# Router logits with the gate weights held in the array: two column halves, a turn back on TensorE, a sum on VectorE

## What is computed

```
x1 = layernorm(x + attention(x))              # 4096 x 512
scores = softmax(x1 @ gate_w.T, axis=-1)      # 4096 x 64: the logits are x1 @ gate_w.T
topk_w, topk_idx = top_k(scores, 6)
# tokens are put into slots of their experts in token order, at most 128 an expert
routed = scatter_add(expert(x1[buf_tok]) * buf_w)
out = layernorm(x1 + routed + shared(x1))
```

## Time and profile before

| what | value |
|---|---|
| median of 3 runs | 951.53 us (951.29 to 953.97) |
| span of the profiled execution | 945.2 us, 15175 instructions |
| PE busy | 918.1 us (97% of the span) |
| DVE busy | 683.3 us (72%) |
| ACT busy | 499.5 us (53%) |
| POOL busy | 460.9 us (49%) |
| mean granted TensorE clock | 0.994 |

### The profile page before, as it was taken

How to read it: one execution, slowest core, us unless ns; L and a number is a source line. 1 busy time by engine, 2 the same in 40 slices (tenths; PEclk the granted TensorE clock), 3 DMA queues, 4 the chain that set the end, 5 groups by cost and what they waited for, 6 DMA issues and landing times. The chain is left out here.

```text
span 945.2 us, 15175 instructions
## 1 busy us (share of the span) xinstructions
PE 918.1 (97%) x4626; PEld 727.5 (77%) x4626; DVE 683.3 (72%) x1250; ACT 499.5 (53%) x1015; POOL 460.9 (49%) x540
## 2 busy tenths in 40 slices
PE   9999999999999999998999999999999999999996
PEld 7788888888888888776787777777777677767875
DVE  7996878879797877987766666665655565636776
ACT  5543434344443535453456665666555566545775
POOL 2002456665656656677135445554545544433564
PEclk9999999999999999999999999999999999999998
DMA  7244735434342516275569999999999999969972
GB/s 209 89 155 121 176 90 158 117 108 132 125 127 75 177 59 204 79 268 173 174 196 302 308 322 322 321 316 318 322 287 307 305 305 303 322 113 392 382 259 111
DMA packets 114190, 203.91 MB, mean 216 GB/s; under 512 B 18496, under 2 KB 56384, under 8 KB 113088
## 3 DMA queue, kind: packets, MB, share of 16 engines
q1 hardware_dynamic: 93584, 159.87, 51.6%
q0 software_dynamic: 19520, 35.75, 16.7%
q10 hardware_dynamic: 1008, 7.34, 2.2%
HBM read 143.03 MB, written 59.88 MB: 215 GB/s over the span
## 5 line engine op out<-in xcount | busy, mean ns | idle before, releaser
L1535 POOL DMA_INDIRECT slot_table<-tokens,slot_of x162 | 181.0, 1118 | 86.7 <-issue 50.3
L1577 POOL DMA_INDIRECT acc_rows<-eo,table_sb x64 | 110.6, 1729 | 172.5 <-ACT eo L888 127.2
L1632 PE MATMUL bank<-x_hi,wqkv_hi 128*128 128x512 f32 x384 | 152.1, 396 | 0.3 <-DVE wqkv_lo L972 0.3
L1632 PE MATMUL bank<-x_hi,wqkv_lo 128*128 128x512 f32 x384 | 150.2, 391 | 0.0
L1632 PE MATMUL bank<-x_lo,wqkv_hi 128*128 128x512 f32 x384 | 150.2, 391 | 0.0
L1404 DVE TENSOR_TENSOR wgu_lo<-wgu,wgu_hi 128x1536 fp32r<-128x1536 f32 x64 | 112.4, 1758 | 48.0 <-ACT wgu_hi L882 48.0
L1632 PE MATMUL bank<-wdn,hid_et 96*128 96x512 f32 x256 | 122.8, 602 | 8.2 <-ACT hid_et L924 8.2
L882 ACT CAST wgu_hi<-wgu 128x1536 fp32r<-128x1536 f32 x64 | 94.5, 1477 | 5.8 <-DMA wgu<-w_gu 5.4
L1566 POOL DMA_INDIRECT xg<-x_rows,table_sb x64 | 74.3, 1162 | 41.3 <-DVE table_sb L1133 22.0
L1632 PE MATMUL bank<-wgu_hi,xgt_hi 128*128 128x384 f32 x256 | 91.4, 357 | 0.0
L1632 PE MATMUL bank<-wgu_hi,xgt_lo 128*128 128x384 f32 x256 | 85.9, 335 | 0.0
(11 more groups left out here) (183 smaller groups left out, 2146.0 us busy)
## 6 DMA issues: line engine op xcount, KB each, us to landing
wgu<-w_gu SPq DMA_DIRECT2D x64, 768.0 KB, 8.5
wdn<-w_down SPq DMA_DIRECT2D x64, 384.0 KB, 8.5
xres<-x SPq DMA_DIRECT2D x32, 256.0 KB, 2.9
x_turned<-x1t SPq DMA_DIRECT2D x32, 256.0 KB
x_rows<-x SPq DMA_DIRECT2D x32, 256.0 KB, 3.0
acc_rows<-x SPq DMA_DIRECT2D x32, 256.0 KB, 3.1
fin<-acc_rows SPq DMA_DIRECT2D x8, 1024.0 KB, 12.1
odd<-acc_rows SPq DMA_DIRECT2D x8, 1024.0 KB, 13.9
```

The source lines that it names most:

```text
L1535: pool.indirect_dma_start(table_dram, bass.IndirectOffsetOnAxis(slot_of[:, i, k:k + 1], 0), tokens[:, i:i + 1], None, bounds_check=SLOTS - ...
L1577: pool.indirect_dma_start(acc_dram[e % 2], bass.IndirectOffsetOnAxis(table_sb[:, e:e + 1], 0), eo[eo_slot[e]][:, :], None, bounds_check=T ...
L1632: mm = pe.matmul(out_ap, a, b, start=first and i == 0, stop=final and i == len(products) - 1)
```

## The change

The roles in `gate` are swapped: a piece of the gate weights (128 x 64) is held in one half of the array's columns and 128 columns of x1t stream through. Pieces 0 and 2 go to columns 0 to 63, pieces 1 and 3 to columns 64 to 127, and the result, 2 halves of 64 experts by 128 tokens, stands turned. ACT copies it to SBUF (`copy_gate`), PE turns it back (`turn_logits`, one transpose of 128 x 128, after project k of the next step), and DVE adds the halves into `logits` (a tensor_reduce, at the head of `top`). With that `top` moves from the end of a step into the next one, ahead of phi_k, and `route` from the start of that step to behind `run_kv`. `count_before` stays where it was. On ACT the exp of the logits becomes `soften`, behind the exp and relu of k, and `scale_score` goes to the end of the step.

```diff
 # PE
+            def turn_logits(i):
+                pe.wait_ge(gate_copied, i + 1)
+                pe.wait_ge(consts, C_IDENT)
+                if i:
+                    pe.wait_ge(logits_done, i)
+                pe.transpose(logits_ps(i), gate_out[:, :], ident[:, :]).then_inc(logits_mm, 1)
...
-                chain(small_ps[:, 0:E], [(x1t_sb[i % 2][:, k, :], gate_sb[:, k, :]) for k in range(KC)]).then_inc(score_mm, 1)
+                for k in range(KC):
+                    half = slice(k % 2 * E, (k % 2 + 1) * E)
+                    mm = pe.matmul(gate_ps[half, :], gate_sb[:, k, :], x1t_sb[i % 2][:, k, :], start=k < 2, stop=k >= KC - 2)
+                mm.then_inc(score_mm, 1)
...
                 project(s, it, c, 0, k_mm)
+                if before_tile is not None:
+                    turn_logits(before_tile)
                 mix(it, c, 0)
...
                 gate(i, 0)
                 if i + 1 < NT:
                     turn_x1(i + 1)
+                turn_logits(i)
                 unit()
 # DVE
             def top(i):
+                dve.wait_ge(logits_mm, i + 1)
...
+                dve.tensor_reduce(logits[:, 0:E], logits_ps(i).rearrange("p (h e) -> p e h", h=2), axis=AX.X, op=ALU.add).then_inc(logits_done, 1)
...
-                if before_tile is not None:
-                    route(before_tile)
                 if s:
                     numerator(s - 1)
                 if s and it + 1 < NB:
                     x_low(it + 1, c)
+                if before_tile is not None:
+                    top(before_tile)
...
                 if s == len(qk) - 1:
                     dve.wait_ge(head_send_done, 1)
+                if before_tile is not None:
+                    route(before_tile)
                 mix(it, c, 1)
...
                     place(before_tile)
-                if tile is not None:
-                    top(tile)
 # ACT
-            def copy_logits(i):
+            def copy_gate(i):
                 act.wait_ge(score_mm, i + 1)
-                act.wait_ge(consts, C_PADS)
                 if i:
-                    act.wait_ge(any_done, i)
-                act.copy(logits[:, 0:E], small_ps[:, 0:E]).then_inc(logits_done, 1)
+                    act.wait_ge(logits_mm, i)
+                act.copy(gate_out[:, :], gate_ps).then_inc(gate_copied, 1)
+
+            def soften(i):
                 act.wait_ge(top_done, i + 1)
...
-                if before_tile is not None:
-                    scale_score(before_tile)
                 if s and it + 1 < NB:
                     split_x(it + 1, c)
...
                 feature_parts(s, 0)
+                if before_tile is not None:
+                    soften(before_tile)
...
                 split_att()
+                if before_tile is not None:
+                    scale_score(before_tile)
                 if tile is not None:
-                    copy_logits(tile)
+                    copy_gate(tile)
```

More of the change, by code:

```diff
@@ L123, in build @@
     att_lo = att.place("att_lo", [P, KC, BT], F32R)
-    den = att.place("den", [P, P])
     rden = att.place("rden", [P, P])
@@ L131, in build @@
     rden_parts = att.place("rden_parts", [P, BT], F32R)
+    gate_out = att.place("gate_out", [P, P])
     logits = att.place("logits", [P, E + 2])
@@ L329, in build, with logits_ps @@
         proj_ps, turn_ps, rows_ps, small_ps, count_ps = banks[0:3], banks[3], banks[4], banks[5], banks[7]
+        gate_ps = banks[5][:, 0:P]
+        def logits_ps(i):
+            return turn_ps[:, 0:P] if i < LAST - 3 else small_ps[:, P:2 * P]
         send_ps = [banks[6], banks[4]]
@@ L840, in _ @@
             rden_high(NB - 1)
+            soften(LAST - 4)
             scale_score(LAST - 4)
             unit()
-            copy_logits(LAST - 3)
+            copy_gate(LAST - 3)
             split_shared(2, "d", sd_hi, sd_stage)
+            soften(LAST - 3)
             copy_turned(LAST - 2)
@@ L848, in _ @@
             split_att()
-            copy_logits(LAST - 2)
+            copy_gate(LAST - 2)
+            soften(LAST - 2)
             divided[0] += 2
@@ L857, in _ @@
             copy_turned(LAST - 1)
-            copy_logits(LAST - 1)
+            copy_gate(LAST - 1)
             apply_x1(LAST)
+            soften(LAST - 1)
             copy_turned(LAST)
@@ L863, in _ @@
             for i in range(LAST, NT):
-                copy_logits(i)
+                copy_gate(i)
                 if i + 1 < NT:
                     copy_turned(i + 1)
+                soften(i)
                 scale_score(i)
@@ L1352, in _ @@
                         split_x1t(0)
+            top(LAST - 4)
             numerator(STEPS - 1)
@@ L1661, in spread, with out_rows @@
                 pe.matmul(send_ps[part % 2][:, :], head_send[:, part, :], rden_parts[:, :], start=True, stop=True).then_inc(send_mm, 1)
-            def out_rows(i):
+            def out_rows(i, chunks=range(KC)):
                 b, j = divmod(i, NJ)
                 tok = slice(j * P, (j + 1) * P)
[L1666 to L1671, removed]
+                if 0 in chunks:
+                    pe.wait_ge(stage_lo, NSTAGE)
+                    if i:
+                        pe.wait_ge(x1_added, i)
+                    pe.wait_ge(div_done, KC * (b + 1))
+                for k in chunks:
                     pe.wait_ge(att_lo_done, KC * b + k + 1)
@@ L1674, in out_rows @@
                                first=k == 0, final=k == KC - 1)
-                mm.then_inc(out_mm, 1)
+                if KC - 1 in chunks:
+                    mm.then_inc(out_mm, 1)
             def sums(b, gated):
@@ L1815, in _ @@
             count_rest(LAST - 5)
+            turn_logits(LAST - 4)
             sums(NB - 1, LAST - 3)
@@ L1820, in _ @@
             gate(LAST - 3, NB)
+            spread(NB - 1, 0)
+            spread(NB - 1, 1)
+            turn_logits(LAST - 3)
             unit()
             count_rest(LAST - 4)
-            spread(NB - 1, 0)
-            spread(NB - 1, 1)
             count_before(LAST - 3)
@@ L1831, in _ @@
             spread(NB - 1, 3)
+            turn_logits(LAST - 2)
             unit()
@@ L1838, in _ @@
             gate(LAST - 1, 0)
-            out_rows(LAST + 2)
+            out_rows(LAST + 2, (0, 1))
+            turn_logits(LAST - 1)
+            out_rows(LAST + 2, (2, 3))
             count_before(LAST - 1)
```

24 lines of the change are left out of this document (16 added, 8 removed).

## The result

The changed kernel takes 991.96 us (median of 5 runs, 985.48 to 995.99), against 953.97 us for the kernel before, measured beside it (median of 5, the three runs of the table above among them): ratio 1.0382, 95% interval 1.0344 to 1.0420, slower. The ratio is taken over all the runs and not from the two medians. The profiled execution is the fastest of the five, 985.48 us with a span of 983.7, so that 1.8 us lie around the span.

The account below looks back on a forecast made before the run. PE, busy 918.1 of 945.2 us, was taken as the bound. Adding 21.6 for block waits, 0 for last tiles and 5 for clock gave a 971.8 us span; with 6.3 for the median, 978 us, range 966 to 996.

Parts of the forecast that it names:

- the sum: Whole kernel: span before 945.2, plus 21.6 for blocks, 0 for last tiles, 5 for clock, giving 971.8 us.
- rival 1: Both waits, and PE loses more: gate halves run serially or clock falls after c=1 too; 988 to 998 us, chance 0.20.
- The gate: Gate on PE: 0.64 us until the next matmul instead of 0.89, a gain of 0.25 us.
- The net gain: Gate's gain less the 0.12 us turn back on PE: 0.13 us a tile, 4.2 us for 32 tiles.
- c=1: Second step of a block: PE waits 1.73 us at count_before, as any_choice now comes behind run_kv.
- c=2: Third step of a block: PE waits 2.26 us more at count_before, between 1.36 and 2.88.
- c=0 and c=3: First and last steps of a block: any_choice is ready in time, so PE has no wait at count_before.
- The clock: Granted clock halves after three of six c=2 waits, costing 5 us (0 to 10).
- The tail: Closing loop: some 2.3 us wait at turn_logits(30) offset by a shorter wait at turn_x1(30); 0, 3 us either side.
- faster: At count_before: any_choice is ready whenever PE comes, and the gate's 4.2 us gain remains; 947 us, chance 0.04.
- VectorE catches up in c=2: DVE's stretch in c=2 shrinks to PE's 10.14 us, only the c=1 wait is left; 960 us, chance 0.10.
- the heavier case: Same as rival 1: serial gate halves (8 us) or clock falls after c=1 waits (up to 10 us); chance 0.20.

Follow-up runs that it names:

- route early: Changed kernel with route on VectorE moved back to right behind phi_k, ahead of run_kv; 960.7 us, ratio 1.0092 to the kernel before.
- route early with the old tail: Changed kernel with route back right behind phi_k, and tiles 25 to 31 using the gate and tail order of the kernel before; 953.04 us, ratio 0.9978.

## Why the prediction was right, and by how much it was off

The direction and the mechanism of the blocks held; the time was 14 us above the forecast of 978 and inside the range. The 14 can be told apart. The span of the profiled run is 11.9 us above the 971.8 of the sum: the blocks with their clock lost 27.25 for 26.6, the tail 13.0 for 0, the experts gave 1.8 back for 0. The run of the median, not profiled, has a span of 990.2, 6.5 more, at a clock of 0.979. Against that, the 6.3 us that were added for what lies around the span were 4.5 too many: here it is 991.96 - 990.2 = 1.8, and 2.0 to 3.5 in the 24 runs of the kernel before beside the last variants. So the first trace of before, with its span of 945.2, came from an execution of some 947 to 949 us, an estimate from these differences, which is faster than the median. 11.9 + 6.5 - 4.5 = 13.9.

That the range held it is in part luck: its high end had 3 us for the tail, and the 13.0 found room in waits of 2.88 us, six falls of the clock and 6 us of rival 1, which did not come in that measure.

- **The gate.** 0.59 us where 0.64 was worked out from `sums`, so the halves do run side by side. But the start behind `count_before` is 0.09 us later, and from `count_before` on the gain is 0.93 - 0.72 = 0.21, for 0.25. The Trainium skill (TensorEngine Tiling (Array Packing), Key Properties) says that changing the tiling mode drains the engine; the later start agrees with that. Its twofold figure (Theoretical Speedup) is not reached: 0.89 to 0.59 is 1.5, and 1.3 with the later start.
- **The net gain.** 0.13 us a tile were taken; route early shows 10.23 - 10.19 = 0.04 in c=1, and 52.01 us for a block (203.68 to 255.69) against 52.27, 0.065 a tile. The turn was priced right: from it to the next projection it is 329.72 - 329.38 = 0.34 with a `spread` between, and a `spread` alone takes 0.23 (311.31 to 311.54 in the trace of before), so 0.11 for 0.12. With the gate's 0.21 that leaves 0.10; where the rest goes isn't shown. Over 25 tiles 0.065 is 1.6 us; the ratio of route early with the old tail, 0.9978, allows from 0 to 4.
- **c=1.** Predicted 1.73 us from start to start; 1.65 in blocks 2, 4 and 7 (1.49 by the view, 1.48 in block 7). In blocks 3, 5 and 6, where the view gives 2.2 us, another thing comes in (last section). The chain was that of the forecast.
- **c=2.** Predicted 2.26 from a stretch of 12.4 us between the `run_kv` ends; it is 235.50 - 223.20 = 12.30, and the wait is 2.10 from start to start, 1.94 by the view in blocks 2, 4, 5 and 6 within 0.01. Block 3 has 1.73 and block 7 2.72.
- **c=0 and c=3.** No wait, as predicted. A block loses 3.45 us for 3.6; the 14 waits sum to 24.8 us for "some 12, about 24", and two of them, 1.5 us, are in the tail.
- **The clock.** Three falls after c=2 waits, as taken, but one also after a c=1 wait: four stretches of 3.4 us at half clock, 6.8 us lost where the term had 5. With two more stretches in the tail it is 8.1 over the span of the profiled run, and more in the others, whose clock is lower. The length of a wait alone does not decide it: of the 1.94 to 1.95 us of c=2, two kept the clock and two didn't.
- **The tail.** This is the step that failed. The working looked at tile 30 alone, and there it was right: PE waits 2.51 us (2.3 predicted) for the copy, which stands behind ACT's `hid_hi`, and the wait of 2.79 us at turn_x1(30) is gone.

```profile
487.74 0.66 PE L1751 MATMUL bank<-ident,x 128*128 128x128 f32 x4
490.90 0.34 PE L1774 MATMUL bank<-ident,gate_out 128*128 128x128 f32 x1 [2.51 <-ACT gate_out L719]
```

What it missed is tiles 25 and 26, whose turn stands behind their own gate with only two spreads (25), or a `count_rest` and two spreads (26), between. Of tile 26, in the trace of after:

```profile
448.39 0.66 PE L1766 MATMUL bank<-x1t,gate_sb 128*64 128x128 f32 x8
...
454.91 0.27 ACT L719 COPY gate_out<-bank 128x128 f32<-128x128 f32 x1 [6.75 <-remote]
...
455.23 0.47 PE L1774 MATMUL bank<-ident,gate_out 128*128 128x128 f32 x1 [5.49 <-issue]
```

ACT has nothing else to do, and yet copies the gate's result 5.86 us after the gate's last record ends (449.05). In the old tail a whole unit follows without a need for that result. From `count_before` of tile 25 to that of tile 26 it is 7.4 to 11.5 us in the five profiles with the old tail and 14.8 to 17.3 in the eight with the new gate there. How much of the 5.49 us PE really stood isn't shown: a late result of this kind comes in the kernel before as well (last section). So 0 was taken for a tail that costs some 8.5 us on one chip, and 13.0 between the two first profiles, where before had the shortest of its tails.

Against the rivals: "faster" decided at the end of `run_kv`, which no part of the change moved, and did not come; "VectorE catches up in c=2" is refuted by the 12.30 us; of the heavier case the fall of the clock after c=1 came once in the profiled run, and the serial halves not at all.

## What to carry to other kernels

When a producer is moved on one engine, take the consumer's place on the other engine, subtract the new end from it, step by step of the schedule, and do the same at every hand-written end of the program: the price stood in two rows of the old trace, and the part that was looked at for one tile only is the part that was missed. Before the span of one execution and the median of others are added up, look whether the difference between them is the same in other runs. A gain on an engine that now waits is no gain until the wait is gone; here one call behind or ahead of two scans was worth 28 to 35 us, the rebuilt gate 2. A wait of 1.5 to 2 us on TensorE costs more than its length, as the clock may halve behind it.

## What the runs showed of the hardware that was not expected

TensorE's results can reach the other engines long after its records end, for some microseconds at a time. The profile models the ends of matmuls, so it may be that the records are early and not the results late. The clearest case is in the second profile of the kernel before itself, in the tail:

```profile
425.01 1.00 PE L1632 MATMUL bank<-gate_sb,x1t 128*128 128x64 f32 x8
...
431.98 0.21 ACT L714 COPY logits<-bank 128x64 f32<-128x64 f32 x1 [7.67 <-remote]
...
433.22 0.20 PE L1700 MATMUL bank<-any_choice,before 128*128 128x64 bf16 x1 [3.88 <-issue]
```

The gate's last record ends at 426.01, ACT idles for 7.67 us and copies its result at 431.98; the granted clock from 425.0 to 433.2 is given as 1.00. A stretch at half clock follows, from 434.4 to 441.2. The same in small lies in the c=1 steps of the changed kernel whose wait is 2.2 and not 1.49 us, here block 6:

```profile
332.53 0.64 PE L1751 MATMUL bank<-ident,x 128*128 128x128 f32 x4
...
333.92 0.59 ACT L707 COPY x1t<-bank 128x512 f32<-128x512 f32 x1 [2.39 <-PE bank L1751]
...
335.74 0.39 PE L1652 MATMUL bank<-x_hi,wqkv_lo 128*128 128x512 f32 x1
...
337.50 0.60 ACT L662 ACTIVATE e<-bank 128x512 f32<-128x512 f32 x1 [2.48 <-PE bank L1652]
...
338.33 0.20 PE L1722 MATMUL bank<-any_choice,before 128*128 128x64 bf16 x1 [2.20 <-DVE any_choice L1109]
```

The last record of `turn_x1` ends at 333.17, and ACT, which stands idle for it, copies 0.75 us later (0.04 in block 4); through `att_hi` and `run_kv` that makes the wait at `count_before` 0.71 us longer. Project q's last record ends at 336.13, exp of q starts 1.37 us later. The starts of the records run on at their usual distance meanwhile, so what the view of waits gives as idle time behind them need not all be idle. It occurs with both gates and with both tails, so it doesn't need the change; in the first profile of before, ACT copies within 0.04 us wherever it stands idle for a gate's result. What delays the results, and whether it is the clock in a form that the granted clock does not show, stays open.
